# A transformer kernel on one core: a third slot for softmax probabilities, work moved from VectorE to GpSimd, and the instruction order planned in short stretches

## The chip, the cores and the metric

The kernel runs on one core of a Trainium2 chip. The metric is the time of one execution on the device, in microseconds. Three runs of the kernel before took 4014.59, 4009.04 and 4006.03 us, so the median is 4009.04 us.

## What is computed

The input `x` holds 64 sequences of 128 positions and 128 features, in float32. It goes through four layers, each with a cross-attention against a context of 77 positions per sequence:

```python
# layer 0: rope attention, causal, 16 heads; rope cross-attention, 16 heads; MLP 128-512-128
x = x + attn(ln(x), ln(x), causal) ; x = x + attn(ln(x), ctx) ; x = x + gelu(ln(x) @ fc1) @ fc2
# layer 1: self-attention and cross-attention, 16 heads; mixture of 8 experts 128-512-128, best 2 of 8
x = x + attn(ln(x), ln(x)) ; x = x + attn(ln(x), ln(ctx)) ; x = x + sum(gate_e * expert_e(ln(x)))
# layer 2: a Mamba-2 block (4 heads of 64, state 128), then cross-attention with 8 heads
z, xBC, dt = rms(x) @ in_proj ; y = scan(silu(conv(xBC)), softplus(dt)) ; x = x + rms(y * silu(z)) @ out_proj
x = x + attn(ln(x), ctx, key mask)
# layer 3: cross-attention with 16 heads and a mask of pairs, then layer norm
return ln(attn(x, ctx, pair mask) + x) * g + b
```

## The kernel before

The 64 sequences are handled in 16 passes of four (`NB`, the index `b` below). A pass is a list of steps, in the order in which layer after layer needs them (`pass_steps`). Four streams (`S`) run side by side: stream 0 has passes 0, 4, 8 and 12, stream 1 has passes 1, 5, 9 and 13, and so on. Each stream has its own tiles, and in the trace the numbers of the tiles are left out (`pr` is `pr0` to `pr3`).

A step uses one to three engines in turn (`parts`). "scores" makes the scores of one sequence on TensorE (L976 the mask, L981 the product), "soft" subtracts the maximum on VectorE (L1371, L1377) and takes the exponential on ScalarE (L1207), "turn" transposes the probabilities on TensorE (L991) and copies them on ScalarE (L1216), "mix" multiplies them with the values (L1003, then L1225), "regroup" turns the heads back (L1011) and divides (L1386, L1387). The scores of 16 heads fill four PSUM banks, and one "soft" has eight heads. Before the scores, "spread" on GpSimd (L1558) writes the keys of one sequence into `kx`, set out so that a product gives each head its own scores. The keys of all four sequences of a pass have a slot there (`NB` slots), while the probabilities have two slots in `pr`: the third "soft" of a stream writes into the slot of the first, and so waits until the first has been turned.

A layer norm is "stats" (VectorE sums at L1319 and L1322, then the sign of the mean and the epsilon at L1330 and L1331, or L1326 to L1328 for the RMS norm; GpSimd the power at L1529 and the shift at L1534), "apply" (ScalarE, L1166) and "norm" (TensorE transposes, L934). The gated rows of the Mamba block are scaled by "gate_norm" on VectorE (L1511). The experts are "up" (L1060, one product of 512 columns for every 128 hidden features) and "down" (L1068, added to `x` at L1432). The experts' weights don't fit beside the rest, so "fetch" loads them for two experts at a time, and only one stream can hold these tiles at a time.

The order of the instructions on each engine is computed when the program is built. `timetable` plays the steps through with the costs in `parts`, and at each point picks for each engine, out of the four streams, the candidate with the lowest key:

```python
key = t + LEAD * work[n][m] - EAGER.get(step[0], 0.0) + (STAY if switch else 0.0)
```

Here `t` is when the step could start, `work` how far its stream has come plus the stream's offset in `PHASES`, `EAGER` a head start by kind of step, and `STAY` what a change of ScalarE's function table costs. The costs and these numbers decide only the order; on the chip each engine runs its list in that order and waits on semaphores. The same timetable picks the PSUM banks.

## Time and profile before

| | |
|---|---|
| median of three runs | 4009.04 us |
| the profiled execution, its own time | 4011.71 us |
| its span, first to last instruction | 4009.9 us |
| mean granted TensorE clock, as a share of 2.4 GHz | 0.978 |
| TensorE matmuls busy | 3694.3 us (92%) |
| ScalarE busy | 2773.7 us (69%) |
| VectorE busy | 2703.0 us (67%) |
| GpSimd busy | 879.0 us (22%) |

An engine is busy while at least one of its instructions runs. Matmuls overlap, so a matmul's mean duration times its count is more than the busy time. In the views below PE is TensorE, PEld its weight loads, DVE VectorE, ACT ScalarE, POOL GpSimd and SP SyncE, whose queue issues the loads and stores.

### The profile page before, as it was taken

The page shows a single profiled execution, that of the slowest core. Times are in us where ns is not written, and L with a number is a line of the kernel's source. Part 1 is how long each engine was busy: PE and PEld are TensorE (multiplying, and loading weights), DVE is VectorE, ACT ScalarE, POOL GpSimd, SP SyncE. Part 2 cuts the span into 40 slices and gives each one's busy share as a digit, 9 for nine tenths or more (in the row PEclk, how much of TensorE's full clock was granted, in tenths as well). Part 3 has the DMA queues.
Part 4 walks back from the last instruction along what each step waited for, and adds up shares of the span by engine and source line. Part 5 has one row for each costly group of instructions (what it writes and reads, how often), then busy time and mean ns, then how long its engine had stood idle before and what let it go on. Part 6 is the DMA issues. An engine that isn't in the chain of part 4 may idle for free.

```text
span 4009.9 us, 86936 instructions
## 1 busy us (share of the span) xinstructions
PE 3694.3 (92%) x32576; PEld 2565.6 (64%) x32576; DVE 2703.0 (67%) x5916; ACT 2773.7 (69%) x4904; POOL 879.0 (22%) x996
## 2 busy tenths in 40 slices
PE   6889999998899989999989998999998989899997
PEld 3556766766566656667656665667765656666665
DVE  8776566575876675756776767565687777666464
ACT  4777767666676767765767776776576777777555
POOL 2121122122212121212321212121232212212121
PEclk9999999999999999999999998999999999999998
DMA  1000010100001000010000100001000000010100
GB/s 63 2 3 24 24 45 22 52 22 10 24 10 31 24 1 26 22 51 22 2 32 10 32 23 3 24 22 51 22 3 31 20 22 22 13 34 12 56 4 6
DMA packets 52615, 92.56 MB, mean 23 GB/s; under 512 B 11816, under 2 KB 35312, under 8 KB 51952
## 3 DMA queue, kind: packets, MB, share of 16 engines
q1 hardware_dynamic: 52208, 87.01, 6.6%
q8 instruction: 271, 4.44, 0.5%
q14 instruction: 136, 1.11, 0.1%
HBM read 82.80 MB, written 4.19 MB: 22 GB/s over the span
## 4 chain that ended last, share of the span: by engine, by line
PE 67%; DVE 19%; ACT 7%; issue 3%; POOL 2%; DMA 1%; SPq 0%; DVEq 0%; ACTq 0%; POOLq 0%
PE ps L991 12%; PE ps L1068 11%; PE ps L1060 10%; PE ps L1003 7%; PE ps L981 5%; DVE pr L1377 5%; DVE mx L1371 5%; PE ps L950 3%; PE ps L1011 3%; PE ps L976 2%; PE ps L1023 2%; ACT pt L1216 2%; PE ps L1035 1%; PE ps L1117 1%; PE ps L959 1%
## 5 line engine op out<-in xcount | busy, mean ns | idle before, releaser
L1371 DVE TENSOR_REDUCE mx<-ps 128x8 f32<-128x616 f32 (+1 forms) x704 | 671.5, 954 | 314.6 <-PE ps L981 296.0
L1216 ACT ACTIVATE pt<-ps 77x512 f32<-77x512 f32 (+1 forms) x1408 | 769.2, 593 | 145.8 <-PE ps L991 143.5
L991 PE MATMUL ps<-k_sb,pr 128*77 128x128 f32 (+1 forms) x5632 | 801.7, 283 | 53.7 <-DVE pr L1377 24.6
L1207 ACT ACTIVATE pr<-pr 128x616 f32<-128x616 f32 (+1 forms) x704 | 588.0, 839 | 333.7 <-DVE pr L1377 331.5
L991 PEld LDWEIGHTS ps<-k_sb,pr 128*77 128x77 f32 (+1 forms) x5632 | 631.5, 147 | 245.2 <-issue 122.0
L1377 DVE TENSOR_TENSOR pr<-ps,mx 128x616 f32<-128x616 f32 (+1 forms) x704 | 671.4, 954 | 74.6 <-PE ps L991 51.3
L1529 POOL TENSOR_TENSOR rstd<-var,k_sb 128x4 f32<-128x4 f32 (+1 forms) x160 | 162.9, 1018 | 1951.2 <-DVE var L1331 1733.9
L1060 PE MATMUL ps<-hT,ew 128*128 128x512 f32 x1024 | 492.6, 610 | 7.9 <-DMA ew<-weights 4.7
L1003 PE MATMUL ps<-pt,v 77*16 77x128 f32 (+2 forms) x11264 | 443.3, 279 | 43.5 <-ACT pt L1216 18.7
L1003 PEld LDWEIGHTS ps<-pt,v 77*16 77x16 f32 (+2 forms) x11264 | 252.5, 98 | 247.2 <-issue 110.1
L1225 ACT ACTIVATE og<-ps 128x256 f32<-128x256 f32 x704 | 264.3, 378 | 201.5 <-PE ps L1003 199.1
L981 PE MATMUL ps<-kx,qT 32*128 32x308 f32 (+2 forms) x2816 | 358.2, 542 | 24.5 <-ACT pt L1216 6.6
L1558 POOL TENSOR_TENSOR kx<-kT,in_tiles 128x308 f32<-128x308 f32 (+1 forms) x384 | 318.9, 830 | 182.0 <-issue 130.0
L1432 DVE SCALAR_TENSOR_TENSOR x<-ps,gates,x 128x128 f32<-128x128 f32 x512 | 144.1, 344 | 264.6 <-PE ps L1068 263.2
L1060 PEld LDWEIGHTS ps<-hT,ew 128*128 128x128 f32 x1024 | 181.0, 194 | 179.8 <-issue 132.7
L1166 ACT ACTIVATE xh<-x,dt_p,rstd 128x128 f32<-128x128 f32 x448 | 184.2, 485 | 96.9 <-POOL dt_p L1534 96.5
L1068 PEld LDWEIGHTS ps<-ew,kx 128*128 128x128 f32 x2048 | 235.2, 192 | 13.1 <-issue 7.6
L1068 PE MATMUL ps<-ew,kx 128*128 128x128 f32 x2048 | 240.7, 276 | 1.6 <-DVE pr L1377 1.5
L1068 PE MATMUL ps<-ew,pr 128*128 128x128 f32 x2048 | 240.6, 276 | 1.1 <-ACT pt L1216 0.6
L1011 PE MATMUL ps<-k_sb,og 128*128 128x128 f32 x1408 | 223.8, 281 | 19.4 <-DVE pr L1377 12.2
L1068 PEld LDWEIGHTS ps<-ew,pr 128*128 128x128 f32 x2048 | 234.1, 192 | 5.7 <-issue 2.2
L1255 ACT ACTIVATE kx<-ps,c_sb 128x512 f32<-128x512 f32 x256 | 167.4, 688 | 100.4 <-PE ps L1060 99.0
(169 smaller groups left out, 4966.1 us busy)
## 6 DMA issues: line engine op xcount, KB each, us to landing
ew<-weights SPq DMA_DIRECT2D x128, 512.0 KB, 4.7
x<-x SPq DMA_DIRECT2D x16, 256.0 KB, 3.1
out<-xh SPq DMA_DIRECT2D x16, 256.0 KB, 2.4
cT<-ctx_cols SPq DMA_DIRECT2D x16, 154.0 KB, 3.2
qT<-mask_pairs SPq DMA_DIRECT2D x16, 154.0 KB, 3.8
kx<-ctx_rows SPq DMA_DIRECT2D x16, 154.0 KB
w_sb<-weights SPq DMA_DIRECT2D x1, 1542.0 KB, 10.7
w_sb<-weights SPq DMA_DIRECT2D x1, 1280.0 KB
```

Source lines behind the costliest of these rows:

```text
L981: i = mm(o, qT[s][r, b * L:(b + 1) * L], spread_keys[s][r, pl.slot(("spread", a, s, b), NB), 0:4 * keys], start=mask is None, stop=True)
L991: i = tr(p[0:keys, j * L:(j + 1) * L], pr[s][:, pl.slot(unit, 2), c:c + keys], ident)
L1003: i = mm(ps[32 * j:32 * j + t.slot, pl.banks[step][0], q * L:(q + 1) * L], heads_of(s, t)[0:keys, n, :], pt[s][0:keys, q, j * L:(j + 1) * ...
L1011: i = tr(p[:, q * L:(q + 1) * L], og[:, s % S, q * L:(q + 1) * L], ident)
L1060: mm(p[:, 0:NB * L], ew[:, e // 2 % 2, 0, e % 2 * FF + c * 128:e % 2 * FF + (c + 1) * 128], hT[s][:], start=True, stop=True)\
L1068: i = mm(p[:, b * D:(b + 1) * D], h1[s][e % 2][:, c * NB * L + b * L:c * NB * L + (b + 1) * L], ew[:, e // 2 % 2, 1, e % 2 * FF + c * D:e ...
L1207: go_act(v, v, ACT.Exp, scale=t.scale).then_inc(probs_ready.sem, 1)
L1216: go_act(pt[s][0:keys, q % 2, :], p[0:keys, :], ACT.Copy).then_inc(probsT_ready.sem, 1)
L1225: go_act(og[:, s % S, 2 * h * L:2 * (h + 1) * L], p[:, 0:2 * L], ACT.Copy)\
L1371: link(v_.tensor_reduce(m, tile, AX.X, ALU.max, negate=True))
L1377: tell(dve, v_.tensor_tensor(dst, tile, m.rearrange("p (c h) -> p c h", c=2).unsqueeze(3).broadcast_to([128, 2, 4, keys]), ALU.add), score ...
L1558: tell(pool, g_.tensor_tensor(spread_keys[s][:, pl.slot(step, NB), 0:4 * keys].rearrange("p (h k) -> p h k", h=4), kT[s][:, b * keys:(b + ...
```

## The change

It has four parts.

1. **Slots.** The first half of each `kx` tile keeps the spread keys, now with two slots instead of four. The second half becomes a third slot for probabilities. "soft" waits for the turn of the "soft" three before it in its stream, not two. "spread" of a sequence waits for the scores of the sequence two before it.
2. **VectorE to GpSimd.** For every "stats" the small operations behind the sums (two for a layer norm, three for the RMS norm) go to GpSimd. "gate_norm" goes there too, as one operation of 128x1024 in place of four of 128x256.
3. **The planner's model.** Some costs in `parts` are changed. TensorE's steps take twice as long in the plan while its modelled clock is at half, and head starts are given by kind and engine, and by attention (`AHEAD`).
4. **The planner's numbers.** `PHASES` are spaced evenly, `STAY` falls from 47.9 to 1.9, and a table `CHANGES` replaces some of the numbers in each stretch of 60 us of the plan.

Cut to its core, the diff is:

```diff
-        return [(V, 1.9 if step[1] == NORM_RMS else 1.6), (G, 1.25)]
+        return [(V, 1.3), (G, 1.5)]
...
-        "gate_norm": [(V, 1.7)], "turn_gate": [(P, 0.11 * NB), (A, act(n, 0.5))],
+        "gate_norm": [(G, 2.0)], "turn_gate": [(P, 0.11 * NB), (A, act(n, 0.5))],
...
     if kind == "spread":
-        return [(None, (t.project, a, s, "k"), None)]
+        return [(None, (t.project, a, s, "k"), None)] + ([(None, ("scores", a, s, args[2] - 2), None)] if args[2] >= 2 else [])
...
-                + ([(V, ("turn", a, s, units[n - 2][0], 2 * units[n - 2][1] + 1), P)] if n >= 2 else []))
+                + ([(V, ("turn", a, s, units[n - 3][0], 2 * units[n - 3][1] + 1), P)] if n >= 3 else []))
...
+def priorities(stretch):
+    change = CHANGES[stretch] if CHANGES else {}
+    eager = {(kind, engine): v for table in (EAGER, change) for kind, by in table.items() if isinstance(by, dict)
+             for engine, v in by.items()}
+    ahead = {**AHEAD, **{a: v for a, v in change.items() if isinstance(a, int)}}
+    return change.get("LEAD", LEAD), change.get("STAY", STAY), eager, ahead
...
+    def at_clock(t, length):
+        pass_windows(t)
+        begin = t
+        while length > 1e-9:
+            rate = 0.5 if half[0] else 1.0
...
-        key = t + LEAD * work[n][m] - EAGER.get(step[0], 0.0) + (STAY if switch else 0.0)
+        key = (t + lead * (work[n][m] + PHASES[n]) - eager.get((step[0], engine), 0.0) - ahead.get(attention_of(step), 0.0)
+               + (stay if switch else 0.0))
...
-LEAD = 0.416394515
-PHASES = (0, 0.280901424, 0.477195298, 0.528231786)
-STAY = 47.9352789
+LEAD = 5.8882751
+PHASES = (0, 0.25, 0.5, 0.75)
+STAY = 1.89020008
...
+STRETCH = 60
+CHANGES = [
+    {0: 5.8, "scores": {P: 1.9}},
+    {"LEAD": 1.02373802},
...
-        spread_keys = Ring([t.rearrange("p (b k) -> p b k", b=NB) for t in flat_kx])
+        spread_keys = Ring([t[:, 0, :].rearrange("p (n k) -> p n k", n=2) for t in kx])
+        probs = Ring([(pr[s][:, 0, :], pr[s][:, 1, :], kx[s][:, 1, :]) for s in range(S)])
...
-                        i = tr(p[0:keys, j * L:(j + 1) * L], pr[s][:, pl.slot(unit, 2), c:c + keys], ident)
+                        i = tr(p[0:keys, j * L:(j + 1) * L], probs[s][pl.slot(unit, 3)][:, c:c + keys], ident)
...
-                    old = pl.earlier(step, 2)
+                    old = pl.earlier(step, 3)
...
-                elif kind == "gate_norm":
-                    (s,) = args
-                    dve.wait_ge(*gate_rstd(s))
-                    for b in range(NB):
-                        i = v_.tensor_scalar(yg[s][:, b, :], yg[s][:, b, :], rstd[s][:, b:b + 1], None, ALU.mult)
-                    tell(dve, i, gate_normed, s)
...
                     pool.wait_ge(*variance(n, s))
-                    i = g_.tensor_tensor(rstd[s][0:m], var[s][0:m], K("half")[0:m], ALU.pow)
...
+                        g_.tensor_scalar(shift[s][0:m], mv[s][0:m, :, 0], -1.0, None, ALU.mult)
+                        link(g_.tensor_scalar(var[s][0:m], mv[s][0:m, :, 1], EPS, None, ALU.add))
+                        link(g_.tensor_tensor(rstd[s][0:m], var[s][0:m], K("half")[0:m], ALU.pow))
...
+                elif kind == "gate_norm":
+                    (s,) = args
+                    pool.wait_ge(*gate_rstd(s))
+                    tell(pool, g_.tensor_tensor(yg[s], yg[s], rstd[s][:].unsqueeze(2).broadcast_to([128, NB, DI]), ALU.mult),
+                         gate_normed, s)
...
-                    old = pl.earlier(step, NB)
+                    old = pl.earlier(step, 2)
```

How the order moves is shown at three places.

SyncE's queue, in the middle of the program, before. A row `out` stores a pass, the three rows behind it load the stream's next pass, `ew` rows are halves of an experts' fetch (eight of them are one pass), and `kx` rows load the context for layer 1:

```order
L891 DMA ew<-weights 128x1024 x10
L882 DMA kx0<-ctx_rows 77x4x128
L904 DMA out<-xh1 128x4x128
L864 DMA x1<-x 128x4x128
L865 DMA cT1<-ctx_cols 128x308
L866 DMA qT1<-mask_pairs 128x4x77
L891 DMA ew<-weights 128x1024 x4
L904 DMA out<-xh2 128x4x128
L864 DMA x2<-x 128x4x128
L865 DMA cT2<-ctx_cols 128x308
L866 DMA qT2<-mask_pairs 128x4x77
L891 DMA ew<-weights 128x1024 x2
```

And the same queue now:

```order
L1190 DMA out<-xh1 128x4x128
L1150 DMA x1<-x 128x4x128
L1151 DMA cT1<-ctx_cols 128x308
L1152 DMA qT1<-mask_pairs 128x4x77
L1177 DMA ew<-weights 128x1024 x4
L1168 DMA kx0<-ctx_rows 77x4x128
L1177 DMA ew<-weights 128x1024 x4
L1190 DMA out<-xh2 128x4x128
L1150 DMA x2<-x 128x4x128
L1151 DMA cT2<-ctx_cols 128x308
L1152 DMA qT2<-mask_pairs 128x4x77
L1177 DMA ew<-weights 128x1024 x4
```

Before, two passes are stored with four halves between them and the next with two. Now there are eight halves, one pass's worth, between a store and the next, and a block of this form comes twelve times in the queue. At the end of the queue pass 12 is now stored with twelve halves still to come and pass 13 with four; before, pass 12 was stored with ten to come and the last three passes behind all of the fetches.

VectorE near the beginning, the first probabilities of streams 0 and 1, before (`pr0` is stream 0's tile; `probs_turned` is the wait for the slot to be free):

```order
L1371 TENSOR_REDUCE mx<-ps 128x8 [waits scores_made,rope_ready]
L1377 TENSOR_TENSOR pr0<-ps,mx 128x1024 [waits probs_turned,dve_link]
L1371 TENSOR_REDUCE mx<-ps 128x8 [waits scores_made,scores_shifted]
L1377 TENSOR_TENSOR pr0<-ps,mx 128x1024 [waits probs_turned,dve_link]
L1358 COPY v1_2<-ps 128x64x8 [waits values_made,scores_shifted]
```

And now:

```order
L1649 TENSOR_REDUCE mx<-ps 128x8 [waits scores_made,values_ready]
L1655 TENSOR_TENSOR kx0<-ps,mx 128x1024 [waits dve_link]
L1649 TENSOR_REDUCE mx<-ps 128x8 [waits scores_made,scores_shifted]
L1655 TENSOR_TENSOR pr0<-ps,mx 128x1024 [waits probs_turned,dve_link]
L1649 TENSOR_REDUCE mx<-ps 128x8 [waits scores_made,scores_shifted]
L1655 TENSOR_TENSOR pr1<-ps,mx 128x1024 [waits dve_link]
```

The third "soft" of stream 0 goes into `kx0` without a wait for a turn, and the fourth goes back to `pr0`.

GpSimd at the end of a pass's Mamba block, before (`kx` rows are "spread", `pr` rows the gate of the scan, `rstd` the power):

```order
L1584 TENSOR_TENSOR pr2<-pr2,pt2 128x512 [waits z_ready,scan_added,keys_spread]
L1538 TENSOR_TENSOR rstd2<-var2,k_sb 128x4 [waits gate_var,scan_gated]
L1529 TENSOR_TENSOR rstd0<-var0,k_sb 128x4 [waits variance,gate_rstd]
L1534 TENSOR_TENSOR dt_p0<-dt_p0,rstd0 128x4 [waits pool_link]
L1548 TENSOR_TENSOR x0<-x0,r_sb 128x512 [waits normed,stats_ready]
```

And now:

```order
L1866 TENSOR_TENSOR pr1<-pr1,pt1 128x512 [waits z_ready,scan_added,scan_gated]
L1840 TENSOR_TENSOR kx3<-kT3,in_tiles 128x512 [waits scores_made,scan_gated]
L1815 TENSOR_TENSOR rstd1<-var1,k_sb 128x4 [waits gate_var,keys_spread]
L1819 TENSOR_TENSOR pr1<-pr1,rstd1 128x1024 [waits gate_rstd]
L1840 TENSOR_TENSOR kx0<-kT0,in_tiles 128x512 [waits scores_made,gate_normed]
L1840 TENSOR_TENSOR kx0<-kT0,in_tiles 128x512 [waits scores_made,keys_spread]
L1808 TENSOR_SCALAR dt_p1<-mv1 128x4 [waits variance,keys_spread]
```

The scaling of the gated rows is new in GpSimd's list, and "spread" rows of other streams stand around it, split into pairs. In ScalarE's list the loads of function tables go from 247 to 294.

## Rows read from the trace of the kernel before

**Rows 1.** The page, busy time, share of the span and instructions.

```profile
PE 3694.3 (92%) x32576; PEld 2565.6 (64%) x32576; DVE 2703.0 (67%) x5916; ACT 2773.7 (69%) x4904; POOL 879.0 (22%) x996
```

**Rows 2.** Stretches of 200 us: length, then busy time (instructions) per engine, TensorE's clock.

```profile
0.00:200.00 200.00, 154.46 (x1424) 94.66 (x1424) 155.08 (x254) 114.14 (x206) 40.63 (x49) 0.99 0.10 32
...
600.00:800.00 200.00, 194.00 (x1571) 137.36 (x1570) 123.62 (x326) 136.74 (x242) 42.77 (x48) 0.99 0.11 37
...
2000.00:2200.00 200.00, 173.16 (x1786) 120.29 (x1785) 140.15 (x289) 136.13 (x266) 42.46 (x52) 0.97 0.07 21
...
2400.00:2600.00 200.00, 183.31 (x1531) 128.99 (x1531) 124.72 (x280) 142.56 (x242) 40.15 (x44) 0.92 0.04 13
...
2800.00:3000.00 200.00, 194.57 (x1673) 139.17 (x1671) 144.21 (x338) 134.00 (x237) 54.35 (x59) 1.00 0.04 12
...
3800.00:4000.00 200.00, 177.41 (x1607) 126.64 (x1605) 118.79 (x290) 117.22 (x219) 45.13 (x50) 0.96 0.03 9
sum 4000.00, PE 3694.28 PEld 2565.57 DVE 2701.78 ACT 2772.03 POOL 875.26; mean PE 184.71 PEld 128.28 DVE 135.09 ACT 138.60 POOL 43.76
```

**Rows 3.** The same stretches, the experts' "up" products (L1060) alone: PE, PEld, clock.

```profile
600.00:800.00 200.00, 46.11 (x96) 17.11 (x96) 0.99 0.11 37
...
2000.00:2200.00 200.00, 7.54 (x16) 2.72 (x16) 0.97 0.07 21
...
2400.00:2600.00 200.00, 22.78 (x48) 8.32 (x48) 0.92 0.04 13
...
2800.00:3000.00 200.00, 21.52 (x48) 8.80 (x48) 1.00 0.04 12
```

**Rows 4.** The nine interior stretches with 48 to 64 "up" products, as one sum.

```profile
sum 1800.00, PE 1683.41 PEld 1174.04 DVE 1212.70 ACT 1284.31 POOL 403.26; mean PE 187.05 PEld 130.45 DVE 134.74 ACT 142.70 POOL 44.81
```

**Rows 5.** Stretches of 50 us: one without experts, and the last two.

```profile
1000.00:1050.00 50.00, 39.97 (x331) 25.36 (x330) 44.44 (x75) 28.07 (x48) 14.54 (x14) 0.88 0.01 3
...
3900.00:3950.00 50.00, 40.43 (x359) 28.14 (x360) 27.54 (x66) 25.29 (x50) 10.94 (x14) 0.86 0.02 6
3950.00:4000.00 50.00, 39.65 (x446) 27.57 (x446) 25.02 (x54) 29.46 (x59) 7.82 (x9) 0.98 0.02 7
```

**Rows 6.** Who waited for whom: us in total, times, longest.

```profile
ACT xh L1166 <- POOL dt_p L1534: 107.6, 65, 5.1
...
DVE pr L1377 <- PE ps L991: 51.3, 26, 8.4
```

**Rows 7.** Groups on VectorE: busy us, mean ns | idle before.

```profile
L1330 DVE TENSOR_SCALAR dt_p<-mv 128x4 f32<-128x4 f32 (+1 forms) x144 | 25.7, 179 | 4.9
...
L1331 DVE TENSOR_SCALAR var<-mv 128x4 f32<-128x4 f32 (+1 forms) x144 | 23.3, 162 | 0.0
...
L1511 DVE TENSOR_SCALAR pr<-pr,rstd 128x256 f32<-128x256 f32 x64 | 18.3, 349 | 0.7
...
L1505 DVE TENSOR_TENSOR var<-var,mv 128x4 f32<-128x4 f32 x16 | 3.3, 209 | 0.5
```

**Rows 8.** Groups on GpSimd.

```profile
L1558 POOL TENSOR_TENSOR kx<-kT,in_tiles 128x308 f32<-128x308 f32 (+1 forms) x384 | 318.9, 830 | 182.0 <-issue 130.0 <-DVE kT L1350 22.7 <-POOL rstd L1538 0.8
...
L1584 POOL TENSOR_TENSOR pr<-pr,pt 128x512 f32<-128x512 f32 x32 | 40.6, 1268 | 229.3 <-DVE pr L1492 173.4 <-issue 48.9 <-POOL pr L1584 4.0
L1568 POOL TENSOR_TENSOR qT<-k_sb,dta 128x512 f32<-128x512 f32 x32 | 33.4, 1043 | 222.1 <-DVE dta L1457 188.9 <-PE ps L1109 33.2
...
L1534 POOL TENSOR_TENSOR dt_p<-dt_p,rstd 128x4 f32<-128x4 f32 (+1 forms) x144 | 29.3, 203 | 11.3
```

**Rows 9.** ScalarE in order of time around a table load: start us, us.

```profile
395.63 1.28 ACT L1207 ACT_TABLE_LOAD   x1
396.93 0.72 ACT L1207 ACTIVATE pr<-pr 128x616 f32<-128x616 f32 x1
```

**Rows 10.** VectorE's L1420, two operands in SBUF: shortest, median and longest.

```profile
L1420 DVE TENSOR_TENSOR tmp<-tmp x16: 424/425/1382, 373.6 to 3711.6; 128x256 f32<-128x256 f32 x16
```

More of the change, by code:

```diff
@@ L398, in streams, with attention_of @@
     return [[step for s in range(n, PASSES, S) for step in pass_steps(s)] for n in range(S)]
+def attention_of(step):
+    return None if step[0] in BY_STREAM + ("stats", "apply", "norm") else step[1]
+def priorities(stretch):
[4 more added lines that the diff above has]
+    return change.get("LEAD", LEAD), change.get("STAY", STAY), eager, ahead
 def timetable(streams):
@@ L423, in timetable, with pass_windows @@
     known = {}
+    half, window, active = [True], [0], [0.0]
+    def pass_windows(t):
+        while (window[0] + 1) * WINDOW <= t:
+            share = active[0] / WINDOW
+            half[0] = share < RISE if half[0] else share < DROP
+            active[0] = 0.0
+            window[0] += 1
+    def at_clock(t, length):
[3 more added lines that the diff above has]
+            rate = 0.5 if half[0] else 1.0
+            d = min(length / rate, (window[0] + 1) * WINDOW - t)
+            active[0] += d
+            length -= d * rate
+            t += d
+            if length > 1e-9:
+                pass_windows(t + 1e-9)
+        return t - begin
     def ready(n, engine, m):
@@ L472, in cost @@
                 beside = sum(free_now[b - 1] + free_now[b + 1] for b in o)
-                return max(clear + HOP, t), beside, -sum(bank_free[b] for b in o)
+                return max(clear + HOP, t), beside, -sum(bank_free[b] for b in sorted(o))
             option = min(banks_of(step), key=cost)
@@ L478, in candidate @@
         switch = engine == A and step[0] in TABLE and table[0] != TABLE[step[0]]
-        key = t + LEAD * work[n][m] - EAGER.get(step[0], 0.0) + (STAY if switch else 0.0)
+        key = (t + lead * (work[n][m] + PHASES[n]) - eager.get((step[0], engine), 0.0) - ahead.get(attention_of(step), 0.0)
+               + (stay if switch else 0.0))
         return key, n, engine, m, step, t, option, switch
+    stretch = 0
+    lead, stay, eager, ahead = priorities(stretch)
     while True:
@@ L489, in timetable @@
                 best[c[2]] = c
-        _, n, engine, m, step, t, option, switch = min(best.values(), key=lambda c: c[5])
+        _, n, engine, m, step, t, option, switch = min(best.values(), key=lambda c: (c[5], ENGINES.index(c[2])))
+        if t >= (stretch + 1) * STRETCH and stretch + 1 < len(CHANGES):
+            stretch += 1
+            lead, stay, eager, ahead = priorities(stretch)
+            continue
         chain = parts(step)
         k = [e for e, _ in chain].index(engine)
-        end = t + chain[k][1] + (SWITCH if switch else 0.0)
+        length = at_clock(t, chain[k][1]) if engine == P else chain[k][1]
+        end = t + length + (SWITCH if switch else 0.0)
         if engine == A and step[0] in TABLE:
@@ L519 @@
 FOREVER = 1e9
-LEAD = 0.416394515
-PHASES = (0, 0.280901424, 0.477195298, 0.528231786)
-STAY = 47.9352789
-EAGER = {"load": 1.5, "stats": -0.3, "apply": -0.2, "bias": -4, "spread": 2.7, "scores": 0.3,
-         "bias_mlp": -0.2, "hidden": 0.4, "context": 4.1, "fetch": -4.6, "down": -0.1, "step_size": 16.4,
-         "step_size2": -8.8, "decay_in": -1.8, "decay": 2.6, "weigh": 3.8, "gate_stats": -0.2,
-         "gate_norm": -10.3, "mamba_out": -0.3, "final": -3.9, "store": -3.7}
+LEAD = 5.8882751
@@ L980, in _ @@
                         r = slice(high * g, high * (g + 1))
-                        i = mm(o, qT[s][r, b * L:(b + 1) * L], spread_keys[s][r, pl.slot(("spread", a, s, b), NB), 0:4 * keys],
+                        i = mm(o, qT[s][r, b * L:(b + 1) * L], spread_keys[s][r, pl.slot(("spread", a, s, b), 2), 0:4 * keys],
                                start=mask is None, stop=True)
@@ L1205, in _ @@
                     act.wait_ge(*scores_shifted(*args))
-                    v = pr[s][:, pl.slot(step, 2), 0:8 * keys]
+                    v = probs[s][pl.slot(step, 3)][:, 0:8 * keys]
                     go_act(v, v, ACT.Exp, scale=t.scale).then_inc(probs_ready.sem, 1)
@@ L1375, in _ @@
                             dve.wait_ge(*probs_turned(*old[1:4], 2 * old[4] + q))
-                    dst = pr[s][:, pl.slot(step, 2), 0:8 * keys].rearrange("p (c h k) -> p c h k", c=2, h=4)
+                    dst = probs[s][pl.slot(step, 3)][:, 0:8 * keys].rearrange("p (c h k) -> p c h k", c=2, h=4)
                     tell(dve, v_.tensor_tensor(
@@ L1558, in _ @@
                     tell(pool, g_.tensor_tensor(
-                        spread_keys[s][:, pl.slot(step, NB), 0:4 * keys].rearrange("p (h k) -> p h k", h=4),
+                        spread_keys[s][:, pl.slot(step, 2), 0:4 * keys].rearrange("p (h k) -> p h k", h=4),
                         kT[s][:, b * keys:(b + 1) * keys].unsqueeze(1).broadcast_to([128, 4, keys]),
```

267 lines of the change are left out of this document (250 added, 17 removed).

## The prediction

> **What bounds the kernel now.** I read the page's busy times first, then a table of 200 us stretches, then the same table for the experts' products alone, and last the waits. The reader is to see in the first that TensorE is the bound: matmuls run in 3694 of 4010 us, 92%, while ScalarE and VectorE stand at 69% and 67% and GpSimd at 22% [rows 1]. So at most 316 us can be won by closing TensorE's gaps, and the rest only by making its work shorter.
>
> The table of stretches says where the gaps are. Over 4000 us TensorE is idle for 4000 - 3694.3 = 305.7 us, of which 45.5 in the first stretch (loads and the first layer norms) and 22.6 in the last [rows 2]. The 18 stretches between them hold 237.6 us, a mean of 13.2 in each. They are far from equal: 26.8 at 2000 and 16.7 at 2400, against 6.0 at 600 and 5.4 at 2800 [rows 2].
>
> The next table gives one reason. The stretch at 600 has 96 of the experts' wide products, that at 2000 has 16 [rows 3]. The experts' phase of a pass needs little of the other engines, attention needs much: at 1000 us, with hardly an expert in flight, VectorE is busy in 44.4 of 50 us and TensorE in only 40.0 [rows 5]. It is tempting to conclude that spacing the passes evenly fills the gaps. The same table speaks against it: the nine interior stretches with 48 to 64 of these products, which is what an even spacing would give everywhere (1024 products over 18 to 20 stretches are 51 to 57), are idle for 1800 - 1683.4 = 116.6 us in all, 13.0 each [rows 4], hardly under the mean of 13.2. Among them are the stretch at 2400 with 16.7 and that at 2800 with 5.4, at 48 products each [rows 2, 3]. So with the same mix the idle time differs by a factor of three. That factor is the fine order: which stream's step stands next in an engine's list when its data come. I take this as what the change can win.
>
> The waits show what a bad neighbour costs. VectorE stands 51.3 us because a "soft" waits for the turn of the one two before it, 26 times [rows 6], and this blocks everything behind it in VectorE's list. ScalarE's "apply" waits 107.6 us for GpSimd's end of the statistics, 65 times [rows 6].
>
> The clock is the other reserve. The mean grant is 0.978, so with two levels, 2.4 and 1.2 GHz, TensorE had 1.2 GHz for 2 x 0.022 = 4.4% of the span, 176 us. The low grants stand in the stretches with gaps (0.92 at 2400, where the idle time is 16.7 us; 1.00 at 2800) [rows 2]. At half speed 176 us hold 88 us worth of full-speed work at most.
>
> **The change part by part.** All sums start from the profiled execution, 4011.7 us with a span of 4009.9; it lies 2.7 us above the median of the three runs.
>
> *Order, even passes and periodic blocks.* SyncE's queue shows that the passes now follow each other with one pass's worth of fetches between them, a block that comes twelve times. An even spacing alone is worth 13.2 - 13.0 = 0.2 us a stretch, about 4 us. The fine order is worth between nothing and the best row: from 13.2 down to 5.4 over 18 stretches is 140 us. The trace of before cannot tell where between, and an order can also be worse: the upper end of idle time at this mix is 16.7, a loss of 18 x 3.5 = 63 us. I take 8.5 us a stretch, nearer to the two good rows (5.4, 6.0) than to the mean, because the mix now never has the expert-free stretches, and because one more slot and a lighter VectorE remove reasons for waits. That is 18 x 4.7 = 85 us won.
>
> *Clock.* If fewer gaps lift the mean grant from 0.978 to about 0.99, matmuls shrink by up to 0.012 x 3694 = 44 us. Part of that time was idle anyway. I take 30; the bounds are 0 and 60.
>
> *Third slot.* It removes waits for turns of 51.3 us on VectorE [rows 6] and gives TensorE more transposes to choose from. Its price is in "spread": of 384 such steps, 192 (sequences 2 and 3) now wait for scores of the same attention. What stands behind them on GpSimd is delayed, above all the statistics of another stream. One spread takes 0.83 us [rows 8], and GpSimd has time for it at 22% busy. The wait that was removed on VectorE partly returns here.
>
> *VectorE to GpSimd.* VectorE loses 144 x (0.179 + 0.162) = 49.1 us, some 9 us for 16 RMS norms (three operations like the 0.209 of L1505), and 18.3 us of gated rows [rows 7]: 76 us, 2.8% of its busy time. GpSimd gains 144 x 2 x 0.203 + 16 x 3 x 0.203 = 68 us of small operations at the price of L1534, and 16 times the gated rows. That 128x1024 operation isn't in the trace; the nearest rows are 128x512 at 1.043 and 1.268 us [rows 8], so it takes 2.1 to 2.5 us against 4 x 0.349 = 1.4 before. In all some 105 us, so GpSimd goes from 879 to about 985 us busy, 25%. The chain of one layer norm grows by 2 x 0.203 - 0.341 = 0.07 us, that of the gate by about 1 us, and 176 of them run beside three other streams. VectorE's 76 us lie beside TensorE except in stretches like that at 1000 us, where it is 89% busy [rows 5]. I take a gain of 15 us for the slot and the moved work together; bounds are -60 (below) and +76.
>
> On a shared resource the trace has a row: VectorE's L1420, with two inputs in SBUF, takes 0.425 us at the median and 1.382 at the longest [rows 10]. The Trainium skill, SBUF — State Buffer, in the section on the doors into it, says that a VectorE operation with two SBUF inputs and a GpSimd operation that reads SBUF exclude each other for a whole instruction. The 1.382 agrees with that. By it, each of the 16 new long GpSimd operations could hold VectorE up once for at most its own length, 16 x 2.5 = 40 us; I leave this in the lower bound, since such VectorE operations are few.
>
> *Table loads.* 47 more, at 1.28 us each and with the next instruction 0.02 us behind [rows 9], are 60 us of ScalarE, which goes from 2774 to 2834 us busy. It is a gap-filler's price: the planner changes tables early to serve whoever is ready. I put 10 us on the path, bounds 0 and 60.
>
> The skill's page ScalarE: Activation LUTs (What ACT_TABLE_LOAD costs) adds a drain of 1.38 us to each switch. This trace doesn't show it: the next instruction follows the load at once. By the page the 47 would be 125 us of ScalarE, and my 10 would be 20.
>
> *Tail.* The last two stretches of 50 us, with two passes left, are idle for 9.6 + 10.4 = 19.9 us in 100 [rows 5], against 6.6 in 100 inside. The new queue finishes passes 12 and 13 earlier, with twelve and four halves still to come, so about 100 us more are run with two passes: +15 us. The same even spacing that helps inside costs here.
>
> *Gates and longer chains:* +5 us.
>
> Sum: -85 - 30 - 15 + 10 + 15 + 5 = -100, so 4011.7 - 100 = 3911.7 for such an execution, and 3909 for the median.
>
> **Rivals.** *The good order everywhere.* The third slot and the planner's knowledge of the clock let every stretch be like the one at 2800, 5.4 us idle at full clock [rows 2]. Then -140 - 50 - 15 + 30 = -175, about 3835. For it: two stretches of before already are like this, at the mix of experts that all will have. Against it: a plan is made with constants, and any wait that it misjudges comes back in each of the twelve blocks.
>
> *The order gives nothing.* The plan improves on its own costs only, and on the chip the stretches stay at 13.0. What is left is -4 for the mix, -15 for VectorE, +15 for the tail and 0 to +5 for tables: about 4009. For it speaks that stretches of one mix differ threefold although one rule made them all, so the plan and the chip do not agree well now.
>
> *GpSimd becomes late: slower.* The mechanism is head-of-line blocking: GpSimd runs its list in order, a "spread" of sequence 2 or 3 waits for TensorE's scores, and behind it stands a layer norm's power of another stream, whose transposes TensorE is to do next. Each of the 160 chains of statistics would be late by a spread and the wait in front of it, 0.83 + about 0.5 us, less what TensorE has to do meanwhile. It decides once the delay is longer than the other streams' ready work. If half of the 160 chains hit TensorE with 1.3 us, that is 104 us, which eats the 100 us won and leaves the tail and the tables: with an order gain of only 40 instead of 85 the time is about 4055. For it: ScalarE already waits 107.6 us on this link [rows 6]. Against it: GpSimd is idle 78% of the time.
>
> **How the numbers follow.** A measurement of this kernel can tell about 0.2%, 8 us, from no change. The forecast at 3909 (say 3865 to 3955) gets 0.57, the good order (3800 to 3865) 0.17, the order that gives nothing or little (3955 to 4020) 0.18, late GpSimd 0.08. Faster by more than 8 us are the first two and 0.11 of the third, 0.85; within it 0.06 of the third; slower 0.01 of the third and the last, 0.09. For eight in ten the range leaves out one in ten on either side: 3825 to 3995.
>
> **What would show it.** Interior 200 us stretches of the new trace idle for 6 to 11 us, fairly equal, with 48 to 60 "up" products in each; mean clock near 0.99; VectorE's busy time down by about 75 us, GpSimd's up by about 100, ScalarE's up by about 60; the wait of "soft" for turns well under 51 us; the new gated rows 2.1 to 2.5 us. The last 150 us should be worse than before. Wrong would be the mechanism if the stretches keep unequal gaps while the time falls, or if PE's busy time, not its idle time, falls most; and the whole if ScalarE's waits for L1534's successor grow over 200 us.

## The result: 3819 us, 4.8% faster, twice the forecast gain

The changed kernel takes 3819.14 us (median of four runs, 3814.6 to 3820.25) against 4007.54 us; the ratio is 0.9524, with a 95% interval of 0.9508 to 0.9541. The forecast was 3909 us with a range down to 3825. The direction came out, and the gain is nearly twice the forecast: 188 us in place of 98.

The page of the changed kernel, its head, against [rows 1]:

```profile
span 3818.3 us, 86916 instructions
...
PE 3622.8 (95%) x32576; PEld 2540.8 (67%) x32576; DVE 2628.9 (69%) x5516; ACT 2835.2 (74%) x4951; POOL 990.7 (26%) x1348
```

The span is shorter by 4009.9 - 3818.3 = 191.6 us. TensorE's busy time fell by 71.5 us, and its idle time from 315.6 to 195.5, by 120.1. VectorE lost 74 us, GpSimd gained 112, ScalarE gained 61, as expected.

Stretches of 200 us of the changed kernel (length, busy time and instructions of PE, PEld, DVE, ACT, POOL, then the clock) answer to [rows 2]:

```profile
600.00:800.00 200.00, 194.93 (x1719) 135.67 (x1716) 140.99 (x303) 154.25 (x269) 58.82 (x78) 1.00 0.06 17
...
2000.00:2200.00 200.00, 195.08 (x1661) 134.60 (x1661) 140.56 (x299) 153.62 (x262) 58.80 (x78) 0.99 0.06 17
...
3600.00:3800.00 200.00, 172.31 (x1336) 121.33 (x1335) 97.24 (x233) 103.47 (x184) 46.26 (x55) 0.92 0.04 13
```

And the middle of the program as one stretch, of the changed kernel:

```profile
400.00:3400.00 3000.00, 2918.66 (x26571) 2061.30 (x26564) 2122.99 (x4493) 2320.05 (x4044) 798.81 (x1087) 1.00 0.08 24
```

and of the kernel before:

```profile
400.00:3600.00 3200.00, 2994.61 (x26318) 2092.12 (x26317) 2160.28 (x4780) 2255.38 (x3968) 701.93 (x792) 0.98 0.07 24
```

The reader is to see two things. Inside, TensorE is now idle for 81.3 of 3000 us, 5.4 in each 200, where it was 205.4 of 3200, 12.8. From 400 to 3400 us the stretches are now about as good as the best one of before. And the matmuls themselves take less busy time: 2918.66 / 26571 = 0.1098 us each against 0.1138, at a mean clock of 1.00 against 0.98.

The stores give a second measure, which turned out to be the useful one. SyncE issues a pass's store when it is done; here are passes 0, 1 and 12 of the changed kernel (start us, us):

```profile
661.14 0.40 SPq L1190 DMA_DIRECT2D out<-xh  x1
892.22 0.40 SPq L1190 DMA_DIRECT2D out<-xh  x1
...
3431.17 0.40 SPq L1190 DMA_DIRECT2D out<-xh  x1
```

and passes 0 and 12 of the kernel before:

```profile
767.55 0.40 SPq L904 DMA_DIRECT2D out<-xh  x1
...
3714.16 0.40 SPq L904 DMA_DIRECT2D out<-xh  x1
```

So the kernel before needed 767.6 us up to the first store, (3714.2 - 767.6) / 12 = 245.6 for each of the next twelve passes, and 295.8 for the rest. The changed one needs 661.1, then 230.8 each, then 387.1. Twelve times 14.7 us are 177 us, nearly the whole gain; the earlier first store (106 us) and the longer rest (91 us) almost cancel.

The waits of the changed kernel (us in total, times, longest) answer to [rows 6]:

```profile
POOL kx L1840 <- PE ps L1267: 741.1, 136, 16.6
...
ACT xh L1452 <- POOL dt_p L1811: 97.9, 67, 4.4
```

GpSimd now waits 741 us for scores before it spreads the next keys, but this costs the others little: the products of the scores wait 8.3 us for L1840, and ScalarE's wait for the statistics went from 107.6 to 97.9 us. VectorE's groups show what the third slot removed, the 51.3 us of waits for turns [rows 6]:

```profile
L1655 DVE TENSOR_TENSOR pr<-ps,mx 128x616 f32<-128x616 f32 (+1 forms) x472 | 450.3, 954 | 16.2
L1655 DVE TENSOR_TENSOR kx<-ps,mx 128x616 f32<-128x616 f32 (+1 forms) x232 | 221.1, 953 | 8.0
```

No releaser is left in these rows. The operations that moved to GpSimd:

```profile
L1808 POOL TENSOR_SCALAR dt_p<-mv 128x4 f32<-128x4 f32 (+1 forms) x144 | 36.2, 251 | 1058.5 <-DVE mv L1608 1057.0
...
L1819 POOL TENSOR_TENSOR pr<-pr,rstd 128x1024 f32<-128x1024 f32 x16 | 30.3, 1894 | 2.2
```

The gated rows take 1.89 us, less than the bounds of 2.1 to 2.5 from rows of half the length.

### The profile page after: what moved, and what is told of

Its sections match the earlier page's. It is cut to its first block, busy times and chain, and to the rows that moved or that the text cites. A ratio compares the mean times of both kernels' runs of the same rounds, so it can differ in the third digit from the quotient of the medians.

```text
span 3818.3 us, 86916 instructions
## 1 busy us (share of the span) xinstructions
PE 3622.8 (95%) x32576; PEld 2540.8 (67%) x32576; DVE 2628.9 (69%) x5516; ACT 2835.2 (74%) x4951; POOL 990.7 (26%) x1348
## 4 chain that ended last, share of the span: by engine, by line
PE 73%; DVE 11%; ACT 7%; POOL 3%; issue 3%; DMA 1%; SPq 1%; DVEq 0%; ACTq 0%; POOLq 0%
PE ps L1277 14%; PE ps L1354 10%; PE ps L1346 9%; PE ps L1289 8%; PE ps L1267 7%; PE ps L1297 3%; PE ps L1236 3%; DVE mx L1649 3%; PE ps L1262 3%; PE ps L1309 2%; ACT pt L1502 2%; DVE pr L1655 2%; PE ps L1245 2%; PE ps L1314 1%; ACT xh L1452 1%
## 5 line engine op out<-in xcount | busy, mean ns | idle before, releaser
L1277 PE MATMUL ps<-k_sb,pr 128*77 128x128 f32 (+1 forms) x3776 | 532.0, 280 | 13.5 <-DVE qT L1628 4.4
L1840 POOL TENSOR_TENSOR kx<-kT,in_tiles 128x308 f32<-128x308 f32 (+1 forms) x384 | 313.5, 817 | 808.9 <-PE ps L1267 741.1
L1493 ACT ACTIVATE pr<-pr 128x616 f32<-128x616 f32 (+1 forms) x472 | 393.3, 841 | 149.7 <-DVE pr L1655 149.0
L1277 PEld LDWEIGHTS ps<-k_sb,pr 128*77 128x77 f32 (+1 forms) x3776 | 416.5, 146 | 117.5 <-issue 71.2
L1655 DVE TENSOR_TENSOR pr<-ps,mx 128x616 f32<-128x616 f32 (+1 forms) x472 | 450.3, 954 | 16.2
L1289 PE MATMUL ps<-pt,v 77*16 77x128 f32 (+2 forms) x11264 | 428.5, 276 | 18.4 <-ACT pt L1502 16.2
L1808 POOL TENSOR_SCALAR dt_p<-mv 128x4 f32<-128x4 f32 (+1 forms) x144 | 36.2, 251 | 1058.5 <-DVE mv L1608 1057.0
L1277 PE MATMUL ps<-k_sb,kx 128*77 128x128 f32 (+1 forms) x1856 | 264.7, 280 | 3.6 <-ACT kx L1493 1.8
L1493 ACT ACTIVATE kx<-kx 128x616 f32<-128x616 f32 (+1 forms) x232 | 194.6, 840 | 67.3 <-DVE kx L1655 66.9
L1277 PEld LDWEIGHTS ps<-k_sb,kx 128*77 128x77 f32 (+1 forms) x1856 | 205.8, 146 | 53.0 <-issue 33.9
```

What stands on the lines that cost most here:

```text
L1277: i = tr(p[0:keys, j * L:(j + 1) * L], probs[s][pl.slot(unit, 3)][:, c:c + keys], ident)
L1289: i = mm(ps[32 * j:32 * j + t.slot, pl.banks[step][0], q * L:(q + 1) * L], heads_of(s, t)[0:keys, n, :], pt[s][0:keys, q, j * L:(j + 1) * ...
L1493: go_act(v, v, ACT.Exp, scale=t.scale).then_inc(probs_ready.sem, 1)
L1655: tell(dve, v_.tensor_tensor(dst, tile, m.rearrange("p (c h) -> p c h", c=2).unsqueeze(3).broadcast_to([128, 2, 4, keys]), ALU.add), score ...
L1840: tell(pool, g_.tensor_tensor(spread_keys[s][:, pl.slot(step, 2), 0:4 * keys].rearrange("p (h k) -> p h k", h=4), kT[s][:, b * keys:(b + 1 ...
```

## The experiments

My theory A was that the fine order wins, by the planner and its numbers; B that the third slot and the lighter VectorE do; C that even passes do. Each time is a median of four or more runs, next to runs of the kernel before on the same chip. All compute the same; only order, slots, engines or the first loads differ. For each I give the three parts told above, as (up to the first store / per pass, the mean of the next twelve / rest), from its own stores in one profiled execution.

**The changed tiles with the old planner.** The old `timetable`, costs and numbers are put back into the changed kernel:

```diff
-LEAD = 5.8882751
-PHASES = (0, 0.25, 0.5, 0.75)
+LEAD = 0.416394515
+PHASES = (0, 0.280901424, 0.477195298, 0.528231786)
... old timetable, EAGER, STAY and costs; no CHANGES
```

> The changed kernel's slots and its work on GpSimd, but the old planner with its old numbers (the old timetable, PHASES, EAGER, STAY, and the old costs of spread, scores and turn). 188 us were won in all. Theory A (the fine order wins: the planner and its numbers): the tiles alone give 5 to 30 us, 3980 to 4005 us, interior 200 us stretches stay at about 12 us idle and unequal. Theory B (the third slot and the lighter VectorE win): at least 90 us, below 3920 us. A slower result would say that numbers tuned for two slots don't fit three.

Measured: 4000.26 us, ratio 0.9975 (0.9964 to 0.9986); (710 / 245.8 / 333). Theory B falls: with the old numbers the slot and the moved work give 10 us. The first store comes 57 us earlier, the passes take what they took, and the rest is 37 us longer.

**The new planner with the old tiles.** Slots, small operations and gated rows are undone:

```diff
-        probs = Ring([(pr[s][:, 0, :], pr[s][:, 1, :], kx[s][:, 1, :]) for s in range(S)])
+        probs = Ring([(pr[s][:, 0, :], pr[s][:, 1, :]) for s in range(S)])
... four slots for keys, statistics and gate_norm on VectorE
```

> The other half: the new planner with its numbers, stretches and clock, but two slots for probabilities, four for keys, and the small operations and gated rows on VectorE, with the planner told so. Theory A: most of the 188 us stays, 3840 to 3900 us. Theory B: most is lost, above 3920 us. A third (the numbers of each stretch fit only the plan they were found with): above 3920 us too, so this run is to be read with the one on two slots alone and the one that shifts the stretches.

Measured: 4213.33 us, ratio 1.0517 (1.0500 to 1.0535); (693 / 260.0 / 381). So theory A as I had it falls too: the new planner and its numbers, without the slot and the moved work, make the kernel 206 us slower than before.

**No stretches.**

```diff
-CHANGES = [ ... ]
+CHANGES = []
```

> The changed kernel with an empty table of stretches: even passes, clock in the plan, one set of numbers for the whole program. Theory A with the stretches as its core: loses 60 to 120 us, 3880 to 3940 us. Theory C (even spacing and the better costs win, the stretches are trimming): loses under 40 us, below 3860 us, interior stretches idle for 6 to 8 us each.

Measured: 3894.20 us, ratio 0.9717 (0.9702 to 0.9731); (690 / 232.5 / 411). The stretches are worth 75 us. Against the changed kernel that is 29 us to the first store, 12 x 1.7 = 20 us in the passes and 24 us in the rest. Its middle is idle for 91.7 of 3000 us:

```profile
400.00:3400.00 3000.00, 2908.28 (x26203) 2034.75 (x26196) 2097.77 (x4425) 2293.50 (x3997) 793.75 (x1075) 1.00 0.07 24
```

**The same order, the moved operations on VectorE.** Order, banks and slots are those of the changed kernel, and each operation stands in VectorE's list where the plan had it:

```diff
+        for step, by in self.begins.items():
+            if step[0] == "gate_norm":
+                by[V] = by.pop(G)
... and the small operations behind bn_aggr on VectorE again
```

> The changed kernel's order, banks and slots to the letter, but the small operations of the statistics and the gated rows are issued on VectorE again, at the same places of the order (76 us more for VectorE, about 110 us less for GpSimd). Theory A: VectorE has slack at 69%, the loss is under 20 us, 3820 to 3840 us. Theory B: 40 to 80 us, 3860 to 3900 us.

Measured: 3821.72 us, ratio 0.9534 (0.9519 to 0.9548); (661 / 231.4 / 384). VectorE is busy for 67 us more, and the time doesn't change beyond its interval:

```profile
PE 3617.9 (95%) x32576; PEld 2538.3 (66%) x32576; DVE 2696.3 (71%) x5916; ACT 2835.4 (74%) x4951; POOL 873.9 (23%) x996
```

**Two slots, planned anew.** Only the slots are undone, the rest stays:

```diff
-                    old = pl.earlier(step, 3)
+                    old = pl.earlier(step, 2)
... and in inputs_of, probs and spread_keys
```

> The changed kernel with two slots for probabilities and four for keys, planned anew with the same numbers; the work on GpSimd stays there. The earlier run with old tiles took 4213 us. If the slots are what these numbers cannot do without, this run is near 4213 us too (above 4100). If it was VectorE's 76 us or the gated rows that broke that plan, it stays below 3950 us.

Measured: 4179.62 us, ratio 1.0439 (1.0421 to 1.0457); (702 / 261.3 / 336). Eleven of the twelve passes take 249.7 us on the mean, the twelfth 389. So the slots are worth 360 us under the new numbers. The run with all the old tiles took 4213.33 us, so the moved work, planned anew, is worth 34 us at two slots. One stretch of it:

```profile
1200.00:1400.00 200.00, 185.40 (x1637) 126.33 (x1636) 141.16 (x286) 145.86 (x250) 47.66 (x65) 0.99 0.05 18
```

With an even mix (51 of the "up" products) TensorE is idle for 14.6 us in it, as in the rows of before.

**Stretches of 62 us instead of 60.**

```diff
-STRETCH = 60
+STRETCH = 62
```

> The changed kernel with the same table, but each set of numbers holds for 62 us of the plan instead of 60, so that by the end the table is two stretches late. Theory A1 (each stretch's numbers fit the few steps they were found on): the gain of the stretches, 75 us, is lost and more, 3890 us or above. Theory A2 (the numbers fit a phase of the program, and the phases come back with each pass): under 30 us lost, below 3850 us.

Measured: 3881.70 us, ratio 0.9693 (0.9677 to 0.9709); (678 / 232.0 / 416). Between the two, nearer to "fitted to a sequence of steps": 63 us of the 75 are gone. The profiled execution is 60 us longer, 17 before the first store, 14 in the passes and 29 in the rest.

**A plan that knows no slow clock.**

```diff
-            rate = 0.5 if half[0] else 1.0
+            rate = 1.0
```

> The changed kernel planned as if TensorE always had its full clock. In the first 400 us and at the end, where the clock does fall, the plan then differs from the chip, and as the order is chosen step by step, a small difference early gives another order later. If the numbers fit a phase, little is lost (below 3850 us); if they fit one sequence of steps, 3890 us or above, as with shifted stretches.

Measured: 3878.14 us, ratio 0.9680 (0.9666 to 0.9695); (706 / 229.6 / 412). The passes are as good as ever; the 59 us lie at both ends, 45 and 25 us in the profiled execution, less 15 won in the passes. Whether the ends suffer because the clock is planned wrongly there, or because any other plan there would do worse with these numbers, this run can't tell.

**No stretches, the old offsets.** Against the kernel without stretches:

```diff
-PHASES = (0, 0.25, 0.5, 0.75)
+PHASES = (0, 0.280901424, 0.477195298, 0.528231786)
```

> The kernel without stretches (3894 us), with the old offsets 0, 0.28, 0.48, 0.53 in place of 0, 0.25, 0.5, 0.75. My reading of the rows of before was that even passes are worth some 5 us by themselves: then 3890 to 3910 us. The rival (even spacing keeps attention of all four streams from falling together, where VectorE is full): 3940 us or more, with stretches idle for 20 us and a lower clock.

Measured: 4087.73 us, ratio 1.0204 (1.0188 to 1.0219); (777 / 245.8 / 361). With these head starts, uneven passes cost 194 us, not 5: 87 up to the first store and 160 in the passes, less 50 in the rest. That seemed to establish theory C.

**The old numbers in the new planner**, with the old offsets:

```diff
-LEAD = 5.8882751
+LEAD = 0.416394515
... old PHASES, STAY and EAGER, no AHEAD, no CHANGES; the clock and the new costs stay
```

> The changed kernel's slots, its work on GpSimd and its new planner (clock, new costs), but the old numbers: old offsets 0, 0.28, 0.48, 0.53, LEAD 0.42, STAY 47.9, old head starts, no stretches. The passes come unevenly again. The same tiles with the old planner took 4000 us. If the planner's model (its clock and costs) is what won, this is below 3950 us; if the numbers won, 3980 to 4030 us.

Measured: 3975.52 us, ratio 0.9916 (0.9898 to 0.9934); (727 / 247.7 / 281), a little under the 3980 that the numbers' side expected. Clock and costs in the planner may be worth some 25 us against the first run, no more.

**The same with even offsets.**

```diff
-PHASES = (0, 0.280901424, 0.477195298, 0.528231786)
+PHASES = (0, 0.25, 0.5, 0.75)
```

> As the run before it, with one line changed: offsets 0, 0.25, 0.5, 0.75, after which the queue of loads and stores is even. My prediction said that even passes are worth some 5 us by themselves. If that holds: within 20 us of the run with old offsets. The rival from the run without stretches and with old offsets (194 us slower than with even ones): at least 60 us faster, 3880 to 3940 us, at old head starts.

Measured: 4067.49 us, ratio 1.0144 (1.0127 to 1.0161); (739 / 247.7 / 356). Neither side had this: even passes make the kernel 92 us slower here. The passes take what they took, 247.7 us, the first store comes 12 us later, and the end is longer by 75 us. That the end of an even plan is longer because it runs with fewer streams is my reading; no run isolates it. Theory C by itself falls.

**Even offsets and LEAD, without head starts.**

```diff
-EAGER = {"stats": {G: -0.5}, "rope": {V: -1}, ...}
-AHEAD = {2: 0.2, 4: 0.2}
+EAGER = {}
+AHEAD = {}
```

> The kernel without stretches (3894 us), with the head starts (EAGER, AHEAD) emptied too, so that only LEAD, STAY and even offsets are left. If even passes and the third slot make the gain: below 3920 us. If it is the fine order by kind of step: above 3960 us.

Measured: 4115.64 us, ratio 1.0268 (1.0253 to 1.0283); (686 / 249.4 / 437). The head starts are worth 221 us on top of the third slot, even passes and the new `LEAD` and `STAY`.

**The first weights last.** In the changed kernel, the first layers' weights are loaded after the small tables and have a semaphore of their own:

```diff
-            sp.dma_start(w_sb[:, 0:W_L1], weights[:, 0:W_L1]).then_inc(fetched, 16)
             sp.dma_start(mk8[:], mask_keys.broadcast_to([128, LC])).then_inc(fetched, 16)
             sp.dma_start(b2_sb[:], expert_b2).then_inc(fetched, 16)
+            sp.dma_start(w_sb[:, 0:W_L1], weights[:, 0:W_L1]).then_inc(fetched_first, 16)
```

> The changed kernel with the first layers' weights (1.28 MB, so far the eighth load) issued last of the first loads and waited for only by TensorE's first product; statistics and transposes of the first passes no longer wait for them. The order is the same. In the trace of before the first layer norm begins at 16 us and the first product at 23 us, while the loads had all landed at 15 us. Expected: the first product 5 to 8 us earlier and the time 4 to 8 us lower, about 3813 us; the rival (the first products aren't on the path of the end, or the weights now land later than 20 us): no change, 3819 us.

Measured: 3819.10 us, ratio 0.9527 (0.9512 to 0.9541): no change. The first product starts 3.8 us earlier, in the changed kernel at

```profile
22.96 2.05 PE L1236 MATMUL ps<-hT,w_sb 128*128 128x512 f32 x2 [0.96 <-ACT hT L1473]
```

and here at

```profile
19.21 2.05 PE L1241 MATMUL ps<-hT,w_sb 128*128 128x512 f32 x2 [0.96 <-ACT hT L1478]
```

but the first store comes 4.4 us later, at 665.6 us. This order doesn't hand on a head start of 4 us; why not, the run doesn't show.

**Only the first twelve stretches.**

```diff
+CHANGES = CHANGES[:12] + [{}]
```

> The changed kernel with its table cut after the first twelve stretches (720 us of the plan); then one set of numbers to the end. By the times of the stores, the 73 us between the kernel without stretches and the changed one are 29 us up to the first store (690 against 661 us), 19 us over the next eleven passes (232.6 against 230.9 us each) and 25 us after the twelfth. So this run should store its first pass near 661 us and take 3894 - 29 = 3865 us. The rival (a plan's later part doesn't keep what an early part gains, because the streams meet in another way): 3880 us or more.

Measured: 3882.38 us, ratio 0.9674 (0.9659 to 0.9688); (663 / 232.9 / 424). The first store comes nearly as in the changed kernel, 27 us earlier than without stretches, but only 12 of them are left at the end: the passes took 4 us more and the rest 13. Here the later part of the plan didn't keep all that the early part gained.

**Two slots with the old numbers**, in the new planner: the edit of the two-slot run above, on the run with old numbers.

> The new planner with the old numbers (3976 us with three slots), now with two slots for probabilities and four for keys; the small operations and the gated rows stay on GpSimd. The slots were worth 360 us under the new numbers. If that is what a slot is worth on this chip: above 4150 us. If the worth of a slot depends on numbers found with it, and these were found with two: 3980 to 4010 us.

Measured: 4017.48 us, ratio 1.0013 (1.0003 to 1.0023); (795 / 244.6 / 293). Here the slots are worth 42 us, not 360. With two slots the first store comes 68 us later and the rest is 13 us longer, and the passes are faster, by 12 x 3.1 = 37 us.

**LEAD by 5%**, in the kernel without stretches:

```diff
-LEAD = 5.8882751
+LEAD = 6.2
```

> The kernel without stretches (3894 us) with LEAD 6.2 in place of 5.89 and nothing else. It measures how far the time scatters between orders that follow from nearly the same numbers. If 3894 us is a broad optimum: 3885 to 3910 us. If it is one lucky order out of a scatter as wide as the runs with shifted stretches suggest: 3930 us or more.

Measured: 3954.08 us, ratio 0.9856 (0.9838 to 0.9873); (694 / 235.9 / 425). One number moved by 5% costs 60 us, 41 of them in the passes. Its steady part, the eleven stretches of 200 us from 1000 us on, as one:

```profile
1000.00:3200.00 2200.00, 2106.59 (x18936) 1471.70 (x18934) 1526.31 (x3188) 1639.91 (x2876) 573.19 (x782) 0.99 0.07 23
```

and the same of the changed kernel:

```profile
1000.00:3200.00 2200.00, 2140.72 (x19458) 1509.17 (x19457) 1556.00 (x3290) 1708.13 (x2978) 590.27 (x802) 1.00 0.07 24
```

TensorE is idle for 93.4 us of the first and 59.3 of the second, 8.5 and 5.4 in each 200.

**What follows.** The table has all kernels, with their time per pass and TensorE's idle time in each 200 us of the same eleven stretches. "New head starts" stands for `EAGER` and `AHEAD`; where they are old, `LEAD` and `STAY` are old too, except in the row without head starts.

| kernel | third slot | even passes | new head starts | us per pass | idle in 200 us |
|---|---|---|---|---|---|
| before | no | no | no | 245.6 | 13.5 |
| two slots, old numbers | no | no | no | 244.6 | 13.8 |
| new tiles, old planner | yes | no | no | 245.8 | 13.2 |
| new planner, old numbers | yes | no | no | 247.7 | 13.4 |
| the same, even offsets | yes | yes | no | 247.7 | 13.1 |
| even offsets, no head starts | yes | yes | no | 249.4 | 15.5 |
| new numbers, old offsets | yes | no | yes | 245.8 | 13.7 |
| new plan, old tiles | no | yes | yes | 260.0 | 15.4 |
| two slots, new numbers | no | yes | yes | 261.3 | 14.9 |
| LEAD by 5% | yes | yes | yes | 235.9 | 8.5 |
| first twelve stretches | yes | yes | yes | 232.9 | 6.1 |
| no stretches | yes | yes | yes | 232.5 | 6.1 |
| stretches of 62 us | yes | yes | yes | 232.0 | 6.1 |
| same order, operations on VectorE | yes | yes | yes | 231.4 | 6.1 |
| changed | yes | yes | yes | 230.8 | 5.4 |
| first weights last | yes | yes | yes | 230.5 | 5.4 |
| full clock in the plan | yes | yes | yes | 229.6 | 5.3 |

Every kernel with all three has 230 to 236 us per pass and 5 to 9 us idle, every one that lacks at least one has 245 to 261 and 13 to 16. With these numbers, taking away any one of the three loses the gain in the steady passes: each was taken away by itself, the slot from the changed kernel, the other two from the one without stretches, and each removal costs more (13 us a pass or more) than the one nudge of a number, `LEAD` by 5% (3.4). What the runs don't show is that the three are needed in themselves. The new numbers may only fit the tiles and offsets that they stand with in the changed kernel; no other numbers were tried for two slots or for uneven passes, and one nudge is a thin measure of how far orders scatter. `LEAD` and `STAY` were not varied apart from the head starts either, beyond these 5%. My reading of why the three meet is only argued: a steady block of one pass's work can repeat only when the passes are evenly spaced; a "soft" can be issued a whole step earlier in that block only with a free slot; and the head starts are what places the steps so.

## Why the prediction was right in direction and too small

- **What bounds the kernel.** Right. TensorE's gaps closed, from 316 to 196 us, and its share rose to 95%.
- **Where the size was missed.** The sum had 100 us, 70 of idle time and 30 of busy time; for the profiled executions the gain is 191.6, 120.1 and 71.5. So 50 us of the miss are idle time and 41.5 busy time. Two terms of the sum were too small, the order and the clock.
- **Order term.** This step failed in its size. It asked what a 200 us stretch would be idle for, had rows from 5.4 to 16.7 at the same mix, and took 8.5, a value in the middle, 85 us won. Measured are 5.4 in the middle of the program, which by the same sum is 18 x 7.8 = 140 us. The rows were right and the bound of 140 was too; the choice in the middle had nothing behind it but the scatter of the old stretches. The prediction itself said that the new queue repeats a block twelve times, and the new stretches lie much closer together (3.4 to 7.3 us idle from 800 to 3400 us, against 5.4 to 26.8 before). But a repeating plan doesn't have to be a good one: with even passes `LEAD` at 6.2 gives 8.5 us, the very value of the forecast, and the plan without head starts 15.5. What the trace of before couldn't tell is which block the planner's numbers had found. The rival with the good order everywhere, at about 3835 us and a chance of 0.17, is the nearest to what happened.
- **Even spacing.** "About 5 us by itself" missed the sign in the one run that has it by itself: with the old numbers it costs 92 us, 75 of them at the end, and in the steady stretches the idle time stays (13.1 for 13.4 us). With the new numbers it is worth 194 us. That its worth hangs on the other numbers I did not see.
- **Clock.** I took 30 us with bounds 0 and 60, and the busy time fell by 71.5. The mean grant rose to 0.989, so the time at 1.2 GHz fell from 176 to 2 x 0.011 x 3818 = 84 us. Half of the difference, 46 us, is what the clock can explain, and the traces bear it out: in the stretches at 1.2 GHz the matmuls were busy for 154.3 us before and for 62.4 now, and half of that difference is 46 us too. So this term was sized at 30 and is 46. The remaining 25 us of busy time have another cause, for which the sum had no term. The kernel without stretches, with the same grant of 0.989, is busy for 3655.2 us, 32 more than the changed one, and has 65.8 us of it at 1.2 GHz, so under 2 of the 32 us are the clock's. The order changes the busy time without the clock. Overlap of neighbouring matmuls and their weight loads is a candidate that I haven't isolated, and as the profile models the ends of matmuls, part of it may be the model's.
- **Third slot.** I gave it, with the moved work, 15 us (bounds -60 and +76). By itself it has no price: 42 us under the old numbers, 360 us under the new. Under the old numbers, slot and moved work together give 10 us in the old planner, near the 15.
- **VectorE to GpSimd.** Cost and busy times were right (74 us against 76, 112 against 105; three operations of 0.209 us for 16 RMS norms are 10 us, not 9). The worth of the move in the same order is 3 us, within the uncertainty. Planned anew with two slots it is 34 us.
- **The shared port.** The 40 us of the lower bound never arose, but the two engines did hold each other up. VectorE's L1420 of [rows 10] was long three times before (1145, 1372 and 1382 ns). Each time it began while a GpSimd operation of 128x512 was running, and ended 0.28 us behind it, as here:

```profile
1741.80 1.37 POOL L1588 TENSOR_TENSOR xh<-xh,r_sb 128x512 f32<-128x512 f32 x1 [3.61 <-ACT xh L1173]
1742.08 1.37 DVE L1420 TENSOR_TENSOR tmp<-tmp 128x256 f32<-128x256 f32 x1
```

  In the changed kernel L1420 is L1698, which is never longer than 426 ns. The operation before it in VectorE's list, L1696, also with two inputs in SBUF, is long once (at 3407.8 us, beside a GpSimd operation of 1.33 us), and elsewhere it is GpSimd that waits. Its last operation of the statistics, L1811, takes 202 ns at the median, and 462 to 466 in the five passes in which it starts 0.02 us behind L1698:

```profile
L1696 DVE TENSOR_TENSOR tmp<-tmp,k_sb x16: 424/424/1373, 308.1 to 3591.7; 128x256 f32<-128x256 f32 x16
...
1565.67 0.43 DVE L1698 TENSOR_TENSOR tmp<-tmp 128x256 f32<-128x256 f32 x1
1565.69 0.47 POOL L1811 TENSOR_TENSOR dt_p<-dt_p,rstd 128x4 f32<-128x4 f32 x1
```

  With this the rule of the Trainium skill (SBUF — State Buffer, on the engine ports), that the operation that starts first keeps the other out for a whole instruction, agrees. One pair differs: in eight passes the power on GpSimd, L1810 (1.19 us there, 1.04 at the median), had been running for 0.33 us when L1698 began, and L1698 took its 424 ns all the same. The new gated rows met no VectorE operation with two inputs in SBUF; all 16 took 1.89 us.
- **Table loads.** ScalarE's busy time grew by 61 us as computed. What of it lies on the path no run isolated.
- **Tail and start.** The tail was expected to cost 15 us. The part after the thirteenth store grew by 91 us, but the part up to the first shrank by 106, and I counted one side. How much of either is the offsets' doing is open: even offsets alone cost 12 us at the start and 75 at the end with the old numbers, and with the new ones they win 87 at the start and cost 50 at the end.
- **GpSimd late.** Wrong, and rightly unlikely: its waits for scores, 741 us, fall on an engine with time to spare, and ScalarE's wait for it shrank.

## What to carry to other kernels

When an order repeats in blocks, don't average over the stretches of the old trace: one block then stands for the whole program, so a small difference in it counts twelve times, and the forecast should give the good block everywhere a chance worth naming. How good the block is, the old trace doesn't say. Don't price a buffer or a scheduling number by taking it away alone; a slot was worth 42 or 360 us depending on the numbers around it, and numbers found with it made the kernel 4% slower than before without it. Split a pipelined kernel's time at its stores into start, time per pass and rest: that tells in three numbers where an edit acts.

## What the runs showed of the hardware

VectorE operations with two inputs in SBUF and GpSimd operations that read SBUF held each other up (425 ns became 1382, 202 became 466), but it mattered little: 67 us of VectorE work moved to GpSimd in an unchanged order changed the time by 3 us. And TensorE's busy time isn't a constant of the work: 32576 matmuls took 3622.8 us in one order and 3655.2 us in another, both at a mean grant of 0.989, with 62.4 and 65.8 us of it at 1.2 GHz.
